# First loads of a graph network on two DMA queues, and three reorderings beside them

## The reference, cut to what matters

```python
def reference(x, adj, ...):            # x (16, 512, 128), adj (16, 512, 512)
    x = norm(x + adj @ (x @ W0) + b0)                       # L0, all nodes
    for g, idx in enumerate(GROUPS):                        # L1, nodes 0..24, five groups
        A = adj[:, idx][:, :, idx] + I
        A = A * deg(A)**-0.5 on rows and on columns
        h = relu(A @ (x[:, idx] @ W1[g]) + b1[g])
        fused[:, idx] += softmax(fusion_w)[g] * relu(A @ (h @ W2[g]) + b2[g])
    x = norm(x + fused)
    h = x @ W_w.T + W_b; u = adj * exp(e + f.T + a_b)       # L2, attention over adj
    x = norm(x + (u / u.sum(2)) @ h)
    # L3: convolutions of 1 and 17 taps, message passing with exp(-dist) * adj, a GRU
    return norm(x + L3(x, adj))
```

## Time and profile before

| what | us |
|---|---|
| median of three runs | 573.02 |
| the profiled execution | 571.94 |
| its span, from the first to the last instruction | 570.2 |
| PE busy | 550.7 (97% of the span) |
| DVE busy | 477.9 (84%) |
| ACT busy | 399.0 (70%) |
| POOL busy | 218.5 (38%) |

### The profile page before, as it was taken

How to read it: one execution, slowest core, us unless ns; L and a number is a source line. 1 busy time by engine, 2 the same in 40 slices (tenths; PEclk the granted TensorE clock), 3 DMA queues, 4 the chain that set the end, 5 groups by cost and what they waited for, 6 DMA issues and landing times.

```text
span 570.2 us, 12148 instructions
## 1 busy us (share of the span) xinstructions
PE 550.7 (97%) x3639; PEld 486.2 (85%) x3639; DVE 477.9 (84%) x1768; ACT 399.0 (70%) x844; POOL 218.5 (38%) x213
## 2 busy tenths in 40 slices
PE   6889999999999999999999999999999999999994
PEld 6777898989889898989898898989898988989684
DVE  3887778898888989888888889898888888898665
ACT  2477576777787868687777878686777778786452
POOL 3312125263534434352635344343526353442010
PEclk9999999999999999999999999999999999999999
DMA  7980060020020303030200203030302002000000
GB/s 182 327 281 1 1 202 1 2 79 36 20 93 0 111 0 111 0 111 0 80 32 24 87 0 111 0 111 0 111 0 89 23 23 88 2 20 20 2 20 18
DMA packets 33301, 34.46 MB, mean 60 GB/s; under 512 B 1663, under 2 KB 22531, under 8 KB 33146
## 3 DMA queue, kind: packets, MB, share of 16 engines
q1 hardware_dynamic: 32930, 33.99, 18.8%
q10 hardware_dynamic: 344, 0.15, 0.1%
HBM read 29.74 MB, written 4.39 MB: 60 GB/s over the span
## 4 chain that ended last, share of the span: by engine, by line
PE 86%; DVE 1%; ACT 1%; issue 0%; POOLq 0%; POOL 0%; DVEq 0%
PE bank L265 14%; PE bank L267 14%; PE bank L266 14%; PE pair L265 6%; PE pair L267 6%; PE pair L266 6%; PE bank L1685 5%; PE bank L1696 3%; PE bank L1789 2%; PE pair L1845 2%; PE pair L1777 2%; PE bank L1880 2%; PE bank L1881 2%; PE bank L1884 2%; PE bank L1750 1%; PE bank L1860 1%
## 5 line engine op out<-in xcount | busy, mean ns | idle before, releaser
L1173 POOL TENSOR_TENSOR rs<-ve,neg_half 128x4 f32<-128x4 f32 (+1 forms) x60 | 55.3, 921 | 136.1 <-DVE ve L1409 101.2
L1207 POOL TENSOR_TENSOR P_lo<-P,P_hi 128x512 fp32r<-128x512 f32 x56 | 81.9, 1482 | 49.0 <-ACT P_hi L1246 49.0
L265 PE MATMUL bank<-cd_hi,w_hi 128*128 128x256 f32 x272 | 77.2, 284 | 0.0
L266 PE MATMUL bank<-cd_lo,w_hi 128*128 128x256 f32 x272 | 76.5, 281 | 0.0
L267 PE MATMUL bank<-cd_hi,w_lo 128*128 128x256 f32 x272 | 76.2, 280 | 0.0
L1444 DVE TENSOR_TENSOR P<-bank,aT 128x512 f32<-128x512 f32 x64 | 41.1, 684 | 16.7 <-ACT bank L1232 16.6
L265 PE MATMUL pair<-aT_hi,x_hi 128*128 128x512 f32 x128 | 52.2, 408 | 1.5 <-DVE x_lo L809 1.3
L266 PEld LDWEIGHTS bank<-cd_lo,w_hi 128*128 128x128 f32 x272 | 51.2, 188 | 1.6
L265 PEld LDWEIGHTS bank<-cd_hi,w_hi 128*128 128x128 f32 x272 | 51.3, 189 | 1.4
L267 PEld LDWEIGHTS bank<-cd_hi,w_lo 128*128 128x128 f32 x272 | 51.4, 189 | 0.0
L267 PE MATMUL pair<-aT_hi,x_lo 128*128 128x512 f32 x128 | 50.5, 394 | 0.0
(11 more groups left out here) (384 smaller groups left out, 1695.7 us busy)
## 6 DMA issues: line engine op xcount, KB each, us to landing
adj_nat<-in_adj_dram SPq DMA_DIRECT2D x16, 1024.0 KB, 5.9
x_nat<-in_x_dram SPq DMA_DIRECT2D x16, 256.0 KB, 2.9
xt<-in_x_dram SPq DMA_DIRECT2D x3, 1280.0 KB, 12.2
out_dram<-y_out SPq DMA_DIRECT2D x15, 256.0 KB, 2.3
hw<-in_L_gnn_W_dram SPq DMA_DIRECT2D x2, 640.0 KB, 8.4
xt<-in_L_gnn_conv_w_dram SPq DMA_DIRECT2D x1, 1088.0 KB, 6.8
aT<-in_adj_dram SPq DMA_DIRECT2D x5, 96.0 KB
nat_ih<-in_L_gnn_w_ih_dram SPq DMA_DIRECT2D x1, 384.0 KB, 6.1
```

The lines of the kernel that those rows point to most:

```text
L265: nc.tensor.matmul(o, lh, rh, start=start, stop=False)
L266: nc.tensor.matmul(o, lh, rl, start=False, stop=False)
L1173: g.tensor_tensor(rs[i][:, 0:n], ve[i][:, 0:n], neg_half[:, 0:n], ALU.pow).then_inc(po_rs[i], 1)
L1207: g.tensor_tensor(P_lo[:, mc, :], P[:, mc, :], f(P_hi[:, mc, :]), ALU.subtract).then_inc(po_Plo[mc], 1)
```

## The change

The loads of the first part are split between the queues of SP and ACT, and four things change places.

- SP loads the adjacency of graph 0 in two DMAs of 512 KB (chunks 0 and 1, then 2 and 3), with a semaphore each (`q_adj0`, `adj_in[0]`). It waits for the first half before it issues the ten DMAs of `adjP`. It takes four of the `vrows` loads over from ACT, and waits for the second tile of `xt` before it issues `xP`.
- ACT issues the first tile of `xt` and `hw1` behind its `vrows` and behind a wait for `q_adj0`, and `hw2` with the other two tiles of `xt` between its four copies to `aT_hi` and its copy to `agg_sb`.
- PE transposes the first half of the adjacency for all four banks, then the second half. The output product comes ahead of the transposes of the own rows, which are spread behind it: tile 0 ahead of `vrows`, tile 1 ahead of the first own sums, tile 2 behind the hidden layer of graph 0.
- DVE masks tile 1 behind the statistics of `x1`, and tile 2 behind the normalisation.
- ACT copies the transposed rows in the new order, two of its adjacency copies first.

```diff
@@ SP
-                sp.dma_start(adj_nat[0][:, :, :], adj_v[0]).then_inc(adj_in[0], 16)
+                sp.dma_start(adj_nat[0][:, 0:2, :], adj_v[0][:, 0:2, :]).then_inc(q_adj0, 16)
+                sp.dma_start(adj_nat[0][:, 2:NC, :], adj_v[0][:, 2:NC, :]).then_inc(adj_in[0], 16)
+                sp.wait_ge(q_adj0, 16)
                 rows = a["adj"][1:B].rearrange("(t j) n m -> j n t m", j=PJ)
                 for j in range(PJ):
                     ...
-                sp.wait_ge(adj_in[0], 16)
-                x_tile(0)
-                sp.dma_start(hw1[:, :, :], a["L1_gnn_W1"].rearrange("g i h -> i g h")).then_inc(q_h1, 16)
+                for row, name, n in ((G2, "L3_gnn_bn2_g", 1), (BB2, "L3_gnn_bn2_b", 1), (M2, "L3_gnn_bn2_m", 1),
+                                     (V2, "L3_gnn_bn2_v", 1)):
+                    sp.dma_start(vrows[row:row + n, :], a[name].rearrange("(n d) -> n d", n=n)).then_inc(q_row, 16)
                 ...
-                sp.dma_start(hw2[:, :, :, :], a["L1_gnn_W2"].rearrange("g (h p) o -> p g h o", h=2)).then_inc(q_h2, 16)
-                x_tile(1)
-                x_tile(2)
+                sp.wait_ge(q_xr[1], 16)
@@ ACT
+                def x_tile(t):
+                    act.dma_start(xt[t][:, :, :, :].rearrange("p j c d -> p j (c d)"),
+                                  a["x"][1 + PJ * t:1 + PJ * (t + 1)].rearrange("j (p c) d -> p j (c d)", p=128)).then_inc(q_xr[t], 16)
+                act.wait_ge(q_adj0, 16)
+                x_tile(0)
+                act.dma_start(hw1[:, :, :], a["L1_gnn_W1"].rearrange("g i h -> i g h")).then_inc(q_h1, 16)
                 for mc in range(NC):
                     act.wait_ge(pe_aT[mc], 1)
                     s.activation(aT_hi[:, mc, :], bank[mc][:, :], ACT.Identity).then_inc(q_aThi, 1)
+                act.dma_start(hw2[:, :, :, :], a["L1_gnn_W2"].rearrange("g (h p) o -> p g h o", h=2)).then_inc(q_h2, 16)
+                x_tile(1)
+                x_tile(2)
                 act.wait_ge(pe_agg1, 1)
                 s.activation(agg_sb[:, :], AG_BANK[:, :], ACT.Identity).then_inc(ac_agg1, 1)
@@ DVE
-                dve.wait_ge(q_adjP, 32 * PJ)
-                v.tensor_tensor(AB[0:R, 1:NT, :], adjP[0:R, :, 0:NODES], bc(EY[0:R], PT), ALU.add).then_inc(q_A1, 1)
-                hold(dve, q_A1, 3)
-                mask_blocks(1)
                 inverse_degrees(NODES, 0, NG, 1)
                 ...
-                mask_blocks(2)
+                dve.wait_ge(q_adjP, 32 * PJ)
+                v.tensor_tensor(AB[0:R, 1:NT, :], adjP[0:R, :, 0:NODES], bc(EY[0:R], PT), ALU.add).then_inc(q_A1, 1)
+                hold(dve, q_A1, 3)
+                mask_blocks(1)
                 hold(dve, po_rs[0], 1)
                 ...
                 last.then_inc(dv_x1r, 1)
+                mask_blocks(2)
                 mask_blocks(3).then_inc(q_A5, 1)
@@ PE
+                pe.wait_ge(q_adj0, 16)
+                for mc in range(NC):
+                    for c in range(2):
+                        t_.transpose(bank[mc][:, ch(c)], adj_nat[0][:, c, ch(mc)], ident[:, :])
                 pe.wait_ge(adj_in[0], 16)
                 for mc in range(NC):
-                    for c in range(NC):
+                    for c in range(2, NC):
                         last = t_.transpose(bank[mc][:, ch(c)], adj_nat[0][:, c, ch(mc)], ident[:, :])
                     last.then_inc(pe_aT[mc], 1)
                 ...
-                pe.wait_ge(q_adjP, 32 * PJ)
-                transpose_rows(0)
-                transpose_rows(1)
                 pe.wait_ge(ac_agg1, 1)
                 ...
                 block_rows(0)
+                pe.wait_ge(q_adjP, 32 * PJ)
+                transpose_rows(0)
                 pe.wait_ge(q_row, 16 * 14)
-                pe.wait_ge(q_aPT, 2)
                 t_.matmul(bank[7][:, 0:D], vrows[0:NROWS, :], ident[0:NROWS, :], start=True, stop=True).then_inc(q_cols, 1)
                 pe.wait_ge(q_colsb, 1)
-                transpose_rows(2)
+                transpose_rows(1)
                 own_sums(0)
                 ...
                 last.then_inc(q_hid0, 1)
+                transpose_rows(2)
```

More of the change, by code:

```diff
@@ L309, in network_kernel @@
         q_zero, q_ident, q_bd, q_mask, q_mt, q_gm, q_unit = ready("q_zero q_ident q_bd q_mask q_mt q_gm q_unit")
-        q_cst, q_cst2, q_row, q_adjP, q_xP, q_h1, q_h2, q_ww, q_wt, q_wc2, q_keep = ready("q_cst q_cst2 q_row q_adjP q_xP q_h1 q_h2 q_ww q_wt q_wc2 q_keep")
+        q_adj0, q_cst, q_cst2, q_row, q_adjP, q_xP, q_h1, q_h2, q_ww, q_wt, q_wc2, q_keep = ready("q_adj0 q_cst q_cst2 q_row q_adjP q_xP q_h1 q_h2 q_ww q_wt q_wc2 q_keep")
         q_xr = ready("q_xr0 q_xr1 q_xr2")
@@ L348, in _ @@
                         sp.dma_start(adjP[NODES * j + lo:NODES * j + hi, :, :], rows[j, lo:hi]).then_inc(q_adjP, 16)
-                def x_tile(t):
-                    sp.dma_start(xt[t][:, :, :, :].rearrange("p j c d -> p j (c d)"),
-                                 a["x"][1 + PJ * t:1 + PJ * (t + 1)].rearrange("j (p c) d -> p j (c d)", p=128)).then_inc(q_xr[t], 16)
-                sp.wait_ge(adj_in[0], 16)
-                x_tile(0)
-                sp.dma_start(hw1[:, :, :], a["L1_gnn_W1"].rearrange("g i h -> i g h")).then_inc(q_h1, 16)
+                for row, name, n in ((G2, "L3_gnn_bn2_g", 1), (BB2, "L3_gnn_bn2_b", 1), (M2, "L3_gnn_bn2_m", 1),
+                                     (V2, "L3_gnn_bn2_v", 1)):
+                    sp.dma_start(vrows[row:row + n, :], a[name].rearrange("(n d) -> n d", n=n)).then_inc(q_row, 16)
                 sp.wait_ge(q_zero, 1)
@@ L501, in _ @@
                                      (BB1, "L3_gnn_bn1_b", 1), (M1, "L3_gnn_bn1_m", 1), (V1, "L3_gnn_bn1_v", 1),
-                                     (G2, "L3_gnn_bn2_g", 1), (BB2, "L3_gnn_bn2_b", 1), (M2, "L3_gnn_bn2_m", 1),
-                                     (V2, "L3_gnn_bn2_v", 1), (BIH, "L3_gnn_b_ih", 3), (BHH, "L3_gnn_b_hh", 3)):
+                                     (BIH, "L3_gnn_b_ih", 3), (BHH, "L3_gnn_b_hh", 3)):
                     act.dma_start(vrows[row:row + n, :], a[name].rearrange("(n d) -> n d", n=n)).then_inc(q_row, 16)
@@ L509, in _, with copy_adjacency @@
                     s.activation(aT_hi[:, mc, :], bank[mc][:, :], ACT.Identity).then_inc(q_aThi, 1)
+                act.dma_start(hw2[:, :, :, :], a["L1_gnn_W2"].rearrange("g (h p) o -> p g h o", h=2)).then_inc(q_h2, 16)
+                x_tile(1)
+                x_tile(2)
                 act.wait_ge(pe_agg1, 1)
                 s.activation(agg_sb[:, :], AG_BANK[:, :], ACT.Identity).then_inc(ac_agg1, 1)
[L512 to L517, removed]
+                def copy_adjacency(mc):
                     act.wait_ge(dv_aTlo[mc], 1)
                     s.activation(aT[0][:, mc, :], bank[mc][:, :], ACT.Identity).then_inc(ac_aT[mc], 1)
+                copy_adjacency(2)
+                copy_adjacency(0)
+                copy_rows(0)
+                act.wait_ge(q_cols, 1)
+                s.activation(cols[:, :], bank[7][:, 0:NROWS], ACT.Identity).then_inc(q_colsb, 1)
+                copy_adjacency(1)
+                copy_rows(1)
+                copy_adjacency(3)
                 act.wait_ge(q_U0, 1)
@@ L676, in _ @@
                     rest_of_adjacency(mc)
-                dve.wait_ge(adj_in[0], 16)
+                dve.wait_ge(q_adj0, 16)
                 dve.wait_ge(q_gm, 3)
```

## The result

The changed kernel takes 584.77 us (median of four executions, 581.02 to 586.15) against 572.41 us of the kernel before beside it. Over all executions the ratio is 1.0205, with a 95% interval of 1.0174 to 1.0237 (the two medians alone give 1.0216). That is 12 us more; the forecast was 3.8 more.

A forecast was written before the change was run, and what follows sets the result against it. It took the first part to be bound by PE's wait for the adjacency load, then a chain through POOL's second root. Holding 2.46, output product -0.1 and DVE 1.47 gave +3.8, 576.8 us; range 574.8 to 579.3, 8 in 10 572.3 to 580.5.

The forecast's parts named there:

- The earlier adjacency: Start of PE's work: the 2.27 us gap goes, aT_hi starts 1.53 us sooner and agg_sb could start at 15.06.
- The loads on ACT's queue: ACT ahead of agg_sb: issuing hw2 and two xt tiles holds it until 19.05, 2.46 us later than before.
- The upper bound: ACT's hold at most: xt 1 free between 18.1 and 21.0, xt 2 at 20.2 to 23.1, up to +6.5 us.
- rival 3: PE stands still 4.6 us and its clock falls, costing up to 4 us before U0; 578.8 us, chance 0.22.
- DVE: DVE's moved add and masks make the other graphs' degrees, and so the second root, 1.47 us later, all of which counts.
- The -0.1 for the output product's new place: PE: transposes of tiles 0 and 1 no longer run beside agg_sb but behind the output product, gaining 0.1 us.
- adjP at no cost: New waits of DVE and PE: adjP, issued from about 7, lands between 10 and 17, before it is needed.
- Rival 1: ACT is not held, its queue taking the issues at 0.39 us each; 572.8 us, no change, chance 0.17.
- Rival 2: The whole start is gained: ACT not held and DVE's moved masks fall into a wait; 570.6 us, chance 0.08.

The follow-up runs named there:

- e2: Changed kernel with 72 useless transposes of the identity on PE ahead of its wait for agg_sb; 579.39 us, ratio 1.0110.
- e5: Changed kernel with adjP read from consecutive rows of one graph instead of rows of fifteen graphs; 584.12 us, ratio 1.0203.
- e6: Changed kernel with adjP loaded by three DMAs of 128 partitions instead of ten of 16 and 9; 581.78 us, ratio 1.0148.
- e14: Kernel before with hw2 and two xt tiles issued by ACT ahead of agg_sb, xt 0 and hw1 staying on SP; 573.67 us, ratio 1.0032.
- e4: Kernel before with only the adjacency in two DMAs, adjP behind the first, and PE's transposes by halves; 573.95 us, ratio 1.0017.
- e3: Kernel before with only DVE's order changed (corner add and masks of tiles 1 and 2 moved); 574.14 us, ratio 1.0024.
- e12: Changed kernel with every large load and the four vrows back on SP, adjP behind the first half, orders kept; 572.4 us, ratio 1.0017.
- e1: Changed kernel with the issues of hw2 and xt tiles 1 and 2 put back on SP; 577.7 us, ratio 1.0067.
- e13: Changed kernel with all large loads and four vrows on SP, adjP issued without waiting for the first adjacency half; 572.75 us, ratio 1.0008.
- e9: Kernel before with adjP loaded by three DMAs of 125 partitions and nothing else changed; 573.59 us, ratio 1.0027.

## Why the prediction was wrong in size

The direction, the place and the hold of ACT came as forecast, and each sign named for them is in the trace (the adjacency's transposes even start at 8.2 and not at 9.1). 14.28 us of the profile split into 6.42 of holding, 5.68 of clock (30.05 - 24.37) and 2.18 of order (24.37 - 22.19); the forecast had 2.46, nothing, and 1.37. So two steps failed, the size of the holding and a clock put at nothing, and the clock is the larger miss.

- *The earlier adjacency* was right: transposes without a wait, and the product ended at 13.9 where 15.06 was forecast. Some 0.8 us of that is luck, as the dummies ended sooner (3.37 + 4.95 = 8.3 where they ended at 9.1 before), for which no part of the change gives a reason.
- *The loads on ACT's queue*: the step "I take 19.05, because two issues behind the same three loads are the nearest row" failed. `agg_sb` started at 23.01, and at 21.71 and 21.80 in e2 and e5. The row came from a queue on which small loads and 4.9 us of time stood between `xt` 0 and the first held issue, while the engines moved 356 GB/s. Here 2.9 us lay between them, and with `adjP` beside them the engines moved 133 to 173. The forecast let `hw2` be issued when the last copy to `aT_hi` had ended, 5.3 us behind `xt` 0; it was issued 2.5 us behind it (10.13 - 7.67), 1.4 us before that copy ended (10.91 + 0.62). e6 and e14 take the 12.3 us apart: 4.0 with `hw2` alone ahead on the queue, 5.2 more with `xt` 0 and `hw1` ahead, 2 to 3 more with the slow `adjP` (a rough split, as these kernels differ in a few starts).
- *The upper bound* of the holding, 23.1, met 23.01 by luck. It let the first tile come free with the landing of `hw1`, between 18.1 and 21.0, and the second 2.1 us later. The first came free at 16.88, with the landing of `xt` 0; `hw1` landed later than the bound allowed, at 23.5, and the second issue took 6.06 us and came free just ahead of that. Nor is a landing what every held issue waits for: in e14 both were back at 16.5, before any of the loads ahead had landed (`xt` 0 at 9.99 + 7.4 = 17.4, the first).
- *The clock*, kept apart as rival 3 at 0.22 and put at nothing in the sum, was no rival but a consequence of the forecast itself, whose gap was 4.6 us. That the gap of 2.27 us had left the clock alone was no reason against it: it fell in e4 behind 2.31. And the price of at most 4 us ended at `U0`; the clock stayed low for 20 us of work, and cost 4 to 6 (e2).
- *DVE* was right: +1.47 forecast, +1.73 from the sum to the second root in the changed kernel, e3 (1.74) and e12 (24.61 - 16.53 - 6.35 = 1.73). With the rest of the orders it is 2.1 to 2.2 from `agg_sb` to the loop (e2, e12) where 1.37 was forecast. The -0.1 for the output product's new place was not tested by itself.
- *adjP at no cost* was wrong and hidden: e1 shows it at 21, not between 10 and 17. The bound used 151 GB/s as the slow end for a DMA alone; in e4, where SP's queue alone carries large loads, it moves at 142 to 152, with 2.31 us of waiting.
- Rival 1 is out, since ACT was held; but its price without the hold, no change, is what e12 shows. Rival 2 is out: no kernel here with the earlier adjacency beats the one before. The rows of e12 point to why: DVE's second root comes when it came before, and PE waits for a late `xt` tile ahead of the loop.

Open is why DMAs to 16 or 9 partitions run at half the rate (e5 only excludes their source rows), and by what count a queue holds an issue.

## What to carry to other kernels

An engine that computes pays for each load it issues, and the price grows with what still stands ahead on its queue (4.0 us for two tiles behind one load in e14, 9.2 behind three in e6). So put large loads on an engine that computes nothing, as e12 does, or behind the engine's work on the critical chain, which was not tested here. Where a forecast contains an idle gap of PE, price its clock in the same sum, as far as the low clock lasts and not as far as the gap. And before moving a load later, read what its shape moves per microsecond when little else runs.

## What was not expected of the hardware

- A PE at work does not bring the clock back at once: in the changed kernel it was granted 0.50 for 20 us with PE busy 2.00 of 2.00 us in many windows (40 to 42 above), while in e4 it was back after some 3 us (0.50 in 16 to 18, 0.69 in 18 to 20).
- The length of a single gap does not tell whether the clock falls: behind 2.31 us it fell to 0.50 in e4, and in e13 it was 0.50 from 14 to 16 although no gap there had been longer than 1.53 us since the dummies; gaps of 2.27 us before and of 2.77 us in e9 left it at 1.00.
- Full DMA engines say nothing of their rate: 133 GB/s at a share of 1.05 in the changed kernel, and 387 at the same share in e4.
